# Two graph-attention layers on one core: row statistics of layer two by VectorE with GpSimd roots, another end of layer one, bf16 fills, and a new order of all stages

## The reference

```python
# layer one (8 heads of 32): q = x, k = x2, v given
scores = einsum('hnd,hmd->hnm', q * SCALE, k)
attn = softmax(where(adj > 0, scores, NEG_FILL), axis=-1)
x = layernorm(x + einsum('hnm,hmd->hnd', attn, vv))
# layer two: h = x @ W.T + b, per head s_src and s_dst
e = leaky_relu(s_src[i] + s_dst[j], 0.2)
attn = softmax(where(adj == 0, -1e9, e), axis=1)
x = layernorm(x + elu(einsum('ijh,jhd->ihd', attn, h)))
```

## Time and profile before

| | us |
|---|---|
| median of 3 runs | 341.42 |
| lowest, highest | 338.7, 343.41 |
| the profiled execution, its own time | 341.08 |
| its span, first to last instruction | 339.5 |
| DVE busy in the span | 264.3 |
| PE busy | 223.4 |
| POOL busy | 220.6 |
| ACT busy | 172.6 |
| mean granted clock of TensorE | 0.852 of full |

### The profile page before, as it was taken

The page is one execution under the profiler, slowest core; times in us unless marked ns, Lnnn a source line. Parts: engine busy times, 40 slices in busy tenths (PEclk is TensorE's granted clock), DMA queues, the critical chain, the costliest instruction groups (busy, mean ns, idle before and its releaser), DMA issues.

```text
span 339.5 us, 5180 instructions
## 1 busy us (share of the span) xinstructions
PE 223.4 (66%) x1282; PEld 158.0 (47%) x1282; DVE 264.3 (78%) x760; ACT 172.6 (51%) x473; POOL 220.6 (65%) x354
## 2 busy tenths in 40 slices
PE   0099756648685388688888988761714957758850
PEld 0077433436463156466666755450503734536630
DVE  2998999999999489899999766896416388885981
ACT  4646668352867556668643646200020056764495
POOL 8627867726858776787889771167777777777000
PEclk9999695857799679999999999655585899969995
DMA  7977769945886947453535420024434454554212
GB/s 279 384 193 292 258 209 315 336 163 162 270 298 189 323 160 269 124 156 89 165 93 151 105 70 20 33 84 115 108 108 114 108 141 117 133 146 139 64 36 68
DMA packets 23710, 55.90 MB, mean 165 GB/s; under 512 B 6267, under 2 KB 14587, under 8 KB 21627
## 3 DMA queue, kind: packets, MB, share of 16 engines
q0 software_dynamic: 9392, 29.74, 30.5%
q1 hardware_dynamic: 14283, 25.77, 21.8%
HBM read 51.17 MB, written 4.33 MB: 163 GB/s over the span
## 4 chain that ended last, share of the span: by engine, by line
POOL 13%; PE 12%; issue 12%; DVE 10%; ACT 6%; DMA 2%; DVEq 0%; ACTq 0%; POOLq 0%
POOL e_ring L1214 10%; PE e_po L1612 8%; DMA e_ring<-table,e_col_i 2%; DVE e_left L1931 2%; DVE e_weighted L1931 1%; PE e_pj L1636 1%; POOL e_slot_e L1227 1%; DVE e_y L1658 1%; ACT e_search L1320 1%; DVE e_kept L1693 1%; ACT e_prod L1457 1%; DVE e_run L1893 1%; DVE e_run L1895 1%; DVE e_y L1954 1%; PE e_pt L1623 1%
## 5 line engine op out<-in xcount | busy, mean ns | idle before, releaser
L1214 POOL DMA_INDIRECT e_ring<-in_kv,e_col_i x73 | 71.2, 976 | 32.3 <-issue 16.7
L1214 POOL DMA_INDIRECT e_ring<-table,e_col_i x73 | 70.1, 961 | 23.8 <-issue 22.3
L1612 PE MATMUL e_po<-e_weighted,e_sel_edges 128*128 128x264 f32 x178 | 47.3, 402 | 7.0 <-DVE e_weighted L1931 7.0
L1320 ACT ACTIVATE e_search<-e_search 128x2048 bf16<-128x2048 int32 x16 | 39.9, 2491 | 11.4 <-DMA e_search<-in_adj 7.1
L1612 PEld LDWEIGHTS e_po<-e_weighted,e_sel_edges 128*128 128x128 f32 x178 | 32.7, 195 | 14.0 <-DVE e_weighted L1931 9.0
L1560 PE MATMUL e_pq<-e_left,e_sel_rows 128*128 128x256 bf16 x164 | 35.2, 311 | 0.0
L1693 DVE MAX8 e_kept<-e_search 128x8 f32<-128x1024 f32 x24 | 29.4, 1224 | 0.6
L1612 PE MATMUL e_po<-e_left,e_search 128*128 128x264 f32 x92 | 27.3, 452 | 1.7 <-DVE e_left L1931 1.7
L1931 DVE TENSOR_TENSOR e_weighted<-e_ring,e_pc 128x528 f32<-128x528 f32 (+1 forms) x40 | 26.0, 669 | 2.6 <-PE e_pc L1592 1.9
L1599 PE MATMUL e_po<-e_mean_row,e_diagonal 128*128 128x264 f32 x64 | 22.4, 436 | 8.3 <-DVE e_y L1658 7.9
L1356 ACT ACTIVATE e_diagonal<-e_ident,e_filled 128x128 f32<-128x128 f32 x32 | 12.5, 398 | 28.5 <-DVE e_y L1658 28.1
(11 more groups left out here) (240 smaller groups left out, 586.3 us busy)
## 6 DMA issues: line engine op xcount, KB each, us to landing
e_search<-in_adj SPq DMA_DIRECT2D x16, 1024.0 KB, 7.1
table<-e_hx SPq DMA_DIRECT2D x16, 136.0 KB, 1.8
e_ring<-in_kv SPq DMA_DIRECT2D x1, 2112.0 KB, 13.3
out<-e_prod SPq DMA_DIRECT2D x16, 128.0 KB, 2.3
e_ring<-in_kv,e_col_i POOLq DMA_INDIRECT x73, 4.1
e_ring<-table,e_col_i POOLq DMA_INDIRECT x73, 2.8
e_xres<-in_x SPq DMA_DIRECT2D x2, 384.0 KB, 9.8
e_xres<-in_x SPq DMA_DIRECT2D x1, 512.0 KB, 8.0
```

The costliest lines, as they stand in the source:

```text
L1214: nc.gpsimd.indirect_dma_start(out=rings[layer][:, q % RING[layer], :], out_offset=None, in_=kv if layer == 0 else table, in_offset=bass.I ...
L1320: nc.scalar.activation(val_signs[:, k % 2, :], adj_tile[:, k % 2, :], ACT.Sign, accum_out=signs[:, k:k + 1]).then_inc(s("sgn_ready"), 1)
L1612: last = nc.tensor.matmul(po[n % 2][:, 0:CV], selection(layer, u, 1)[:, 0, :], weighted[plan.weighed_into(b)][:, j * CV:(j + 1) * CV], sta ...
```

## The change

Five things change.

1. **Fills.** The f32 diagonals go. POOL writes a flag, three times in bf16, for each row of four tiles (`filled`, four stages instead of seven); PE turns them (`turn_filled`), ACT copies them (`copy_filled`), and DVE splits the mean row, once a layer, into three bf16 parts in partitions that the flags meet (`split_mean`: three copies and two multiply-adds of 128 x 264). A fill is then one bf16 matmul over three partitions. At the start DVE also sets nine small constants.
2. **Statistics.** In layer two, and for the last two tiles of layer one, DVE takes mean and variance by `bn_stats` and `bn_aggr` (`take_moments`); ACT's `spread_of_b` is gone.
3. **ELU and residual.** max(y, 0) + x is a pass of its own (`plus_x`) that does not wait for ACT; `norm_b` adds the exponential and takes the moments. z stands in `e_xres` instead of `e_y`.
4. **Roots.** For the last four tiles POOL takes the root by a power (`roots`), tile by tile, instead of `guess` and `refine`; the last tile is emitted by DVE.
5. **Order.** The stages have other costs and edges and a new `LATER`, `AHEAD` and `FORESIGHT`. `project` of tile 14 is put behind the turn of tile 15.

```diff
-AHEAD = 11.4
+AHEAD = 13.574
-FORESIGHT = 1.4357
+FORESIGHT = 1.6468
...
-LATER = {("back", 0): -0.93, ("back", 1): 1.71, ("copy_mean", 0): 0.36, ("diagonal", 0): -27.48, ("diagonal", 1): -3.99,
+LATER = {("back", 0): -0.63, ("back", 1): -12.93, ("copy_mean", 0): -1.61, ("copy_mean", 1): 0.05, ("exp", 0): -2.8, ("exp", 1): 10.56,
...
-            put("PE", 1.35 if k < 13 else 2.2, rank - 0.2, ("project", k), ("copy_norm", k), None if bank is None else ("evac", k - 1) if k else ("copy_big", BIG_CHUNKS - 1))
+            put("PE", 1.35 if k < 13 else 2.2, rank - 0.2, ("project", k), ("copy_norm", k), ("turn_norm", NK - 1) if k == NK - 2 else None, None if bank is None else ("evac", k - 1) if k else ("copy_big", BIG_CHUNKS - 1))
...
+def alone(k):
+
+    return k >= len(SLOTS) - 4
...
+                elif stage[0] == "roots":
...
+                    pool.wait_ge(s("z_ready"), NT + k + 1)
+                    pool.wait_ge(s("emitted"), k - 3)
+                    own.did(nc.gpsimd.tensor_scalar(var_eps[:, one], moments[:, k % 4, 1:2], EPS, None, ALU.add))
+                    own.wait()
+                    if k == NT - 1:
+                        nc.gpsimd.tensor_tensor(rstd[:, one], var_eps[:, one], minus_half[:], ALU.pow).then_inc(s("rooted"), 1)
+                        continue
+                    own.did(nc.gpsimd.tensor_tensor(rstd[:, one], var_eps[:, one], minus_half[:], ALU.pow))
+                    own.wait()
+                    nc.gpsimd.tensor_scalar(shift[:, one], moments[:, k % 4, 0:1], rstd[:, one], -1.0, ALU.mult, ALU.mult).then_inc(s("rooted"), 1)
...
-                    nc.scalar.activation(diagonal[:, n % 3, :], ident[:], ACT.Copy, scale=filled[:, at:at + 1]).then_inc(s("diagonal_ready"), 1)
...
-                elif stage[0] == "spread_of_b":
...
-                    nc.scalar.activation(elu[:, k % 2, :], y[:, k % 4, :], ACT.Square, bias=neg_mean[:, one], accum_out=squares[:, one]).then_inc(s("var_ready"), 1)
...
-                    nc.tensor.matmul(po[n % 2][:, 0:CV], diagonal[:, n % 3, :], mean_row[:], start=True, stop=False)
+                    nc.tensor.matmul(po[n % 2][:, 0:CV], filled_rows[i:i + 3, at // 4, :], mean_parts[i:i + 3, :], start=True, stop=False)
...
+            def take_moments(k, z):
+                st.did(v.bn_stats(stats[:, k % 4, :], z))
+                st.wait()
+                v.bn_aggr(moments[:, k % 4, :], stats[:, k % 4, :]).then_inc(s("z_ready"), 1)
...
+                elif stage[0] == "plus_x":
...
+                    st.did(v.scalar_tensor_tensor(out=z, in0=y[:, k % 4, :], scalar=0.0, in1=z, op0=ALU.max, op1=ALU.add))
...
-                    v.scalar_tensor_tensor(out=y[:, k % 4, :], in0=elu[:, k % 2, :], scalar=-1.0, in1=y[:, k % 4, :], op0=ALU.add, op1=ALU.max).then_inc(s("elu_used"), 1)
...
+                    v.scalar_tensor_tensor(out=z, in0=elu[:, k % 2, :], scalar=-1.0, in1=z, op0=ALU.add, op1=ALU.add).then_inc(s("elu_used"), 1)
                     dve.wait_ge(s("elu_used"), k + 1)
-                    with_x(1, k).then_inc(s("z_ready"), 1)
+                    take_moments(k, z)
...
+                elif stage[0] == "split_mean":
...
+                    for j in range(2):
+                        st.did(v.tensor_copy(mean_parts[:], mean_row[:]))
+                        st.wait()
+                        st.did(v.scalar_tensor_tensor(out=mean_row[:], in0=mean_parts[:], scalar=less_mean[:, j:j + 1], in1=mean_row[:], op0=ALU.mult, op1=ALU.add))
+                        st.wait()
+                    v.tensor_copy(mean_parts[:], mean_row[:]).then_inc(s("mean_split"), 1)
```

187 lines of the change are left out of this document (121 added, 66 removed).

## The result

The kernel after takes **344.53 us** (median of 20 runs, 342.32 to 348.38), the one before 341.36 (20 runs, 337.81 to 343.41): ratio **1.0109**, 95% interval 1.0083 to 1.0135. It is slower by 3.2 us by the medians, clear of noise but under the 2% that the forecast took as its measure. The forecast was 338.2, its range 331.5 to 344. The profiled execution took 346.27 us, 1.7 above its median; its span is 344.6, that of before 339.5.

The account below looks back on a forecast made before the run. It took DVE's list to bound layer one, then a chain, POOL's gathers, and DVE again in the tail. From 341.08 us, -0.4 + 1.9 - 1.5 - 0.5 - 2.4 = -2.9 gave 338.2 us, range 331.5 to 344.

Parts of the forecast that it names:

- the tail, "0": Behind the last gather: ACT and DVE's closing 4.6 us become 1.3, but 3.3 us return as DVE work; 0.
- First gather near 219.6: Sign to check: layer two's first gather on POOL starts near 219.6 us; wrong if before 216 or after 224.
- fills: Between layer one's last weights and last sums, one fill on PE falls from about 0.6 to 0.2 us; -0.4.
- The wait at 113 us, -2.4: Layer one: half of DVE's 4.88 us wait for a gathered chunk goes, as the new order asks earlier; -2.4 us.
- The check, -1.5: End of layer one: POOL's repair check no longer delays the last half sums and the scores behind them; -1.5 us.
- split_mean, +1.9: Middle of DVE's layer-one list: five added passes over 264 columns lengthen it; +1.9 us.
- The end of layer one, "-0.5": Projections of tiles 14 and 15 back to back, lighter ACT, against tile 12's projection ahead of the last sums; -0.5 us.
- The faster projections: End of layer one on PE: projections gain 0.9 us if the clock holds; left to the range.
- Beside the gathers, "0": Layer two during the gathers: DVE's added 0.77 us a tile fits its idle time and gathers keep their pace; 0.
- The first: Rival: the new order closes half of DVE's 17.7 us of layer-one holes, giving 331.8 us; chance 27%.
- The third: Rival: TensorE falls to its lower clock from 120 to 213.5 us, up to +17, giving 349 us; chance 7%.
- The second: Rival: DVE's new work costs more than POOL and ACT give, and the 113 us wait stays; 343.3 us, chance 15%.

Follow-up runs that it names:

- tail_by_hand: no_late_roots with the repair word read ahead of the last refine and the tail's stages in another order; 342.68 us, ratio 1.0047 to before.
- pool_op_earlier: The kernel before plus one small memset on POOL behind its other work, held until DVE's seventh refine; 341.91 us.
- before_warm: The kernel before plus spare matmuls in PE's pauses at the end of layer one; 339.82 us, interval 0.9924 to 0.9993.
- pool_op_at_end: The kernel before plus one small memset on POOL behind its other work, held until DVE's last refine, the eighth; 344.57 us.
- no_late_roots: The kernel after with the last four tiles' roots taken in pairs by ACT and DVE, not by POOL; 343.47 us, ratio 1.0055 to before.
- the eight fills: The kernel after with each fill matmul done eight times in the same bank; 350.70 us, ratio 1.0218 to before.
- after_old_table: The kernel after's operations in an order planned with the old table of before, LATER too; 351.87 us, ratio 1.0314 to before.
- projections_together: The kernel before with tile 14's projection behind tile 15's turn, and tile 15's copy behind that projection; 339.91 us, ratio 0.9974.

## Why the prediction was wrong

**The step that failed is the tail, "0".** It followed POOL's roots as far as DVE's last emit and put "the store takes the rest" behind it, as if every engine's end were like before. It missed that POOL, too, has to close: 6.37 us of DRAIN behind its last work. That is worth 3.3 us (1.0102 against 1.0006) by adding such an instruction, and 3.4 us (1.0109 against 1.0008) by taking it out, or 1.8 in the other pair (1.0088 against 1.0035). Of the 6.3 us between forecast and measurement it is thus about half; the other 2.9 are the forecast's gain in layer one, of which the profiled execution shows 0.4 at the first gather, and gives it back beside the gathers. It asked who waits for POOL's roots and found DVE's emit, but not the end of the program. The row was there to be asked for, on the closing line of the kernel, and no rival had it. The rest of that step held: `bn_stats` took 0.43 us and `bn_aggr` 0.18 (0.46 and 0.20 with their waits), the last `bn_aggr` ended 1.4 us ahead of the start of the last emit, DVE had no hole of 2 us, and from the division of tile 10 to the last emit both kernels took 24.5 us. Counted from the last gather the last emit ended 1.1 us later than before, because tile 10 was divided later.

**First gather near 219.6: measured 222.02, and for a mixed reason.** Up to the last division of layer one the forecast had -2.4 us (fills, split, check, wait); measured +0.3. Over all traces with the same stages up to there it comes at 208.6 to 210.0 in the order of before, and at 209.3 to 210.3 in that of after (211.9 in tail_by_hand).
- *The wait at 113 us, -2.4.* DVE's longest wait from 100 to 135 us in two of three other kernels that differ from before only behind that place, pool_op_earlier and before_warm (engine, line, releaser: us, times, longest):

```profile
DVE e_rel L1790 <- PE e_pl L1486: 0.3, 1, 0.3
```
```profile
DVE e_prod L1837 <- issue: 1.6, 1, 1.6
```

  The wait of 4.88 us is 0 us in pool_op_at_end and pool_op_earlier and 1.6 in before_warm. In before DVE had come to the product just ahead of it 3.2 us sooner (112.43 for 115.63 in pool_op_earlier), so most of the wait was time won ahead of it; the last division comes 0.5 to 1.2 us sooner where the wait is short or missing. The forecast took half of 4.9 us, seen in one execution, as a gain.
- *The check, -1.5.* Alone it made the kernel 0.85% slower; with the projections together and spare matmuls no loss is left.
- *split_mean, +1.9.* Its price was right: 0.31 for a copy and 0.49 for a combining pass make 1.9. That it lies on the path is not what the trace without it shows.
- DVE's list grew by 4.7 us up to the last division (183.7 us busy for 179.0), not by 1.9. Part is the same instructions taking longer; here `e_match`, which took 0.34 and 0.24 us before (records on DVE up to 210 us):

```profile
L1845 DVE TENSOR_TENSOR e_match<-e_place_no,e_rel 128x176 f32<-128x176 f32 x1 | 1.3, 1254 | 0.0
L1845 DVE TENSOR_TENSOR e_match<-e_place_no,e_rel 128x80 f32<-128x80 f32 x1 | 1.1, 1080 | 0.0
```

  Four such rows and the sixteen of `e_hit`, each by its own length, make +3.9 us. All four stand beside arithmetic with two inputs on POOL, as the pass in the earlier trace rows does:

```profile
181.95 1.04 POOL L1256 TENSOR_TENSOR e_left<-e_xres 128x512 f32<-128x512 f32 x1
182.00 1.08 DVE L1845 TENSOR_TENSOR e_match<-e_place_no,e_rel 128x80 f32<-128x80 f32 x1
```

  In before two of the four stood beside no work of POOL's, one beside the issue of a gather (0.24 us), and one began together with such arithmetic and was not stretched (0.44). That it is POOL that stretches them was not tried.

**The end of layer one, "-0.5", was too cautious**: from the last division to the first gather 12.6 to 13.6 us became 11.8 at the low clock, and 9.3 at the high one, where before_warm has 11.25. The two projections follow each other as said. The faster projections, left to the range at -0.9, are 2.5 us with the mean's, and come in some executions and not in others. Some executions do start the gathers near the 219.6 us that the forecast named (219.49 in no_late_roots), but by the clock and not by its terms; that agreement is luck.

**Beside the gathers, "0", was off by 1 to 2 us.** The gathers kept their 1.25 us, but the division of tile 10 came 91.2 to 92.5 us behind the first of them in the kernels with the new operations and order (apart from the eight fills), 89.5 to 90.6 in those with the old. New operations in an order by the old numbers, after_old_table, have 94.2, which speaks for the operations. DVE's 6.5 us more in that stretch meet sums that ran at a lower clock: the eighteen ahead of the last turn but one took 7.1 us for 6.5. Which of the two costs it was not separated. In the tail the clock falls again. The same eight sums in before (first) and in after:

```profile
316.13 2.05 PE L1612 MATMUL e_po<-e_weighted,e_sel_edges 128*128 128x264 f32 x8 [0.75 <-DVE e_weighted L1931]
```
```profile
318.99 3.81 PE L1654 MATMUL e_po<-e_weighted,e_sel_edges 128*128 128x264 f32 x8 [1.15 <-DVE e_weighted L1983]
```

They take 3.6 to 3.9 us in every trace with the new operations. The pause just ahead of them is not the whole reason: it was 0.27 us in tail_by_hand, with 3.89 us, and as short as in before in projections_together, with 3.42.

**Rivals.** The first, that the order closes DVE's holes, did come in part: up to the last division DVE pauses 26.0 to 26.6 us in the kernels of after's order that have all its operations, tail_by_hand and the eight fills left aside, and 28.9 to 30.9 in before and its three close copies (pool_op_at_end, pool_op_earlier, before_warm). But DVE's own work grew by as much, so that nothing of it reached the time. The third, TensorE at its lower clock, had a mechanism that is there, at the wrong place: not from 120 to 213.5 us (0.98 and 1.00 became 0.93 and 1.00) but at both ends, where PE has short pauses, and at the end of layer one it costs or gives 2.5 us, not 11 as a whole. The second (343.3 us) had a number near the result by luck: `bn_stats` and `split_mean` cost what the forecast said, and only the gain at 113 us failed to come, as it had it. The fills cost PE 8.5 us for 22.4 and gained nothing that a run shows.

## What to carry to other kernels

Before work is given to an idle engine near the end, look at what that engine does last: ask the closing line of the program for every queue's DRAIN, and count it for the engine that is now last: here 6.37 us for GpSimd. A wait in one profiled execution is a gain only if other executions show it too; profile the kernel again, or forecast nothing for it. Taking work from TensorE, or handing it its work sooner, can lengthen what comes next, because a pause can cost twice: itself, and what stands behind it at half the clock. A few spare matmuls in the pauses cost nothing; they gave 0.4% in one kernel and nothing that is shown in the other.

## What the runs showed of the hardware that was not expected

- GpSimd's closing DRAIN takes 6.36 to 6.38 us in every trace here, from its start or, where it was entered while the last gather still ran, from that gather's end. Its last work was a gather, a root or a memset of one column. The other engines' take 0.05 to 0.09.
- Two executions with the same order, with starts that agree to 0.02 us, can part by the granted clock: 1.21 or 2.23 us for the same projection, 2.5 us at the first gather (no_late_roots and after, which differ only in the tail).
- A scalar read of one word on DVE cost 0.95 us where nothing hid it (no_late_roots), in which the load itself lasts 0.54.
- The same f32 pass of 80 elements on DVE took 0.24 us in before, beside the issue of a gather, and 1.08 in after, beside a two-input pass of GpSimd; that GpSimd is the cause was not isolated.
